# A four-layer block with deformable convolutions on one Trainium2 core: column shifts of the side convolution as transfers, the last layer's results through ScalarE

## The chip, the cores and the metric

One core of one Trainium2 chip runs the kernel, as one program written directly for the engines: TensorE (PE), VectorE (DVE), ScalarE (ACT), GpSimd (POOL) and SyncE (SP) each have their own list of instructions and meet at semaphores. The metric is the device time of one execution in microseconds (us). All data are float32.

## What is computed

The input x has shape 2 × 256 × 64 × 64 (two images, 256 channels). Four layers follow one another:

```
x = xn + proj(attention(xn)) + b,   xn = group_norm(x, 8 groups)      # layer 0
x = x + pe                                                             # layer 1
h = relu(bn1(conv1x1(x, w1)))                                          # layer 2, 64 channels
off = conv3x3(h, woff) + boff            # 27 outputs: 9 (y, x) shifts and 9 masks
h = sum_k w2[k] * bilinear(h, grid + off_k) * sigmoid(mask_k)          # 9 taps
x = relu(bn3(conv1x1(relu(bn2(h)), w3)) + x)
h = relu(group_norm(x, 32 groups))                                     # layer 3, 256 channels, twice:
off = conv1x1(depthwise7x7(h, dw), pw) + pwb                           # 18 outputs
h = sum_k w[k] * bilinear(h, grid + off_k) + b                         # 9 taps
return x + (h after the second deformable convolution)
```

## The kernel before

**Stages.** After attention (the first half of the span) there are six gather stages, each over one image of 4096 pixels in 8 groups of 512: two of 64 channels (`copies64`, `sums64`, `products64`: image 1, then image 0), two of the first 256-channel deformable convolution ("layer 0" in the code: images 1 and 0) and two of the second ("layer 1": images 1 and 0). Between them all five engines meet (`meet`), and in the meeting DVE turns the offsets into row numbers and corner weights for the next stage (`corners64`, `corners256`) and makes the group norm's statistics (`group_norm`, bn_stats on L1597, sixteen of 128x512).

**A gather stage of 256 channels.** POOL fetches, by indirect transfers from a table in DRAM, for each pixel and tap one row of four corners, 4 KB (L698). For each of 9 taps, in halves: ACT multiplies the first corner by its weight into the PSUM tensor `ps` (`products`, L1433); DVE adds the other three (`sampled`, L1979) and writes the sampled tile; PE transposes it (L1130); ACT copies the transposed tile out (`staged`, L1445); PE multiplies it with the tap's weights (L1140) and adds up nine taps in two banks of `ps`. PE needs DVE's half (`half_done`) before it transposes it; DVE needs two products of ACT (`prod_ready`) for each half. At the end of a group PE signals `o_ready`, and the result is taken out of `ps`: in layer 0 by ACT, right behind its tap 1 of the next group (`output`, L1454); in layer 1 by DVE, between the two halves of its tap 1, together with the bias and the residual in one instruction (`output`, L1966). Results leave by SP (`group_done`, L480), the residual is fetched by SP in the meeting before (L474).

**Side work.** While a stage gathers from one image, it prepares the next one: normalised rows go to a table in DRAM (ACT `side_normal`, PE `side_table3`, ACT `side_copy3`, SP `table_writes` L368, eight transfers of 64 KB a group), and the 7x7 depthwise and 1x1 convolutions, merged, give the offsets. PE multiplies all 7 rows (`side_rows3`, L1029) into 126 = 7 × 18 rows of `ps` bank 4, one for each of seven column positions and 18 outputs; DVE shifts them (`side_shifts`: one tensor_scalar L1874 and six scalar_tensor_tensor L1880, each of which picks by a 0/1 column of `sel_s` the rows of one column position, shifts them by up to three pixels and adds them into `T3`); PE sums the seven positions and brings pixels onto partitions (`side_shifted`, L976: four small matmuls); DVE adds the base grid (`side_offsets3`, L1890). The last stage (image 0, layer 1) has no side work. The 64-channel stages do the same with three column positions and 27 outputs in the first; in the second, side work is that of 256 channels for image 1.

**Order.** Each engine's list is written out by hand: `nine` for the nine taps of a group, `four` for the four tiles of 128 pixels of a group in the 64-channel stages, and `beside(n, k, ...)` places a piece of side work at tap or tile k. The side work that belongs to the group before (shifts and offsets) is done inside the next one, and behind the loop for the last. In `sums64`, DVE multiplies the gathered rows by their weights (`weigh`, L1916) three tiles ahead of the sum with the residual (`residual`, L1927). ReLU follows in the meeting (half of it `relu_half` on DVE, L2011, half on ACT), and SP spills the residual (`keep_residual`, L462).

## Time and profile before

| | |
|---|---|
| median of 3 runs | 5708.35 us (5702.64 to 5710.03) |
| profiled execution, own time | 5707.99 us |
| its span | 5705.9 us |
| PE busy | 5071.9 us, 89% |
| DVE busy | 4164.4 us, 73% |
| POOL busy | 3185.3 us, 56% |
| ACT busy | 2280.4 us, 40% |
| gathers (q0): packets, MB, share of 16 DMA engines | 193536, 679.59, 31.6% |

The span is the time between the first and the last instruction in the trace; the busy shares are averages over stages with different limits, and DMA runs only in the second half. The six gather stages lie at 2890 to 3284, 3316 to 3725, 3753 to 4228, 4257 to 4734, 4759 to 5291 and 5305 to 5703 us.

### The profile page before, as it was taken

The numbers are of one execution on the slowest core, as the hardware profiler recorded it, in microseconds if no ns is written. First come the engines' busy times: TensorE is split into PE (matmuls) and PEld (weight loads), VectorE is DVE, ScalarE is ACT, GpSimd is POOL, SyncE is SP. The second block draws the span as 40 slices with busy tenths as digits, with TensorE's granted clock in tenths as the row PEclk, the third lists the DMA queues.
The fourth block names the chain that finished last, engine by engine and source line by source line (L and its number), as shares of the span: only waits on it lengthen the run. The fifth ranks groups of instructions, "written<-read, shape, count | busy, mean of one in ns | idle before, by whom it ended". The sixth has DMA issues, their size and how long they took to land. (4 is left out here: it accounts for less than half of the span.)

```text
span 5705.9 us, 75751 instructions
## 1 busy us (share of the span) xinstructions
PE 5071.9 (89%) x23148; PEld 2362.7 (41%) x23148; DVE 4164.4 (73%) x6804; ACT 2280.4 (40%) x4146; POOL 3185.3 (56%) x2819
## 2 busy tenths in 40 slices
PE   7999999998999999999868859959968996889688
PEld 3333333333433333333346646635534553444344
DVE  4888888884588888888433333368878886877798
ACT  2444444442344444444211111135535553444455
POOL 0666666664166666666357657546635653554575
PEclk9999999999999999999978879979989997999899
DMA  2000000001000000000134344379959997897899
GB/s 71 1 1 1 1 1 1 1 1 61 1 1 1 1 1 1 1 1 1 52 99 116 92 148 149 118 288 387 378 220 369 391 370 277 323 353 296 350 409 363
DMA packets 318094, 812.22 MB, mean 142 GB/s; under 512 B 69966, under 2 KB 137428, under 8 KB 317582
## 3 DMA queue, kind: packets, MB, share of 16 engines
q0 software_dynamic: 193536, 679.59, 31.6%
q1 hardware_dynamic: 124302, 129.39, 6.7%
q8 instruction: 140, 2.29, 0.2%
q14 instruction: 116, 0.95, 0.0%
HBM read 708.40 MB, written 100.43 MB: 142 GB/s over the span
## 5 line engine op out<-in xcount | busy, mean ns | idle before, releaser
L646 POOL TENSOR_TENSOR arena<-arena 128x512 f32<-128x512 f32 x960 | 1405.4, 1464 | 829.2 <-ACT arena L1261 764.7
L1261 ACT ACTIVATE arena<-ps 128x1024 f32<-128x1024 f32 x1024 | 1048.6, 1024 | 1240.0 <-PE ps L824 1210.1
L1765 DVE TENSOR_REDUCE arena<-ps 128x2 f32<-128x1024 f32 x1024 | 1243.8, 1215 | 347.3 <-PE ps L798 347.1
L698 POOL DMA_INDIRECT arena<-corners,arena x1152 | 1084.4, 941 | 734.1 <-DVE arena L1979 360.3
L1979 DVE SCALAR_TENSOR_TENSOR ps<-arena,ps 128x256 f32<-128x256 f32 x2304 | 956.7, 484 | 273.3 <-DVEq L1973 264.1
L1140 PE MATMUL ps<-arena 128*128 128x512 f32 x2304 | 1072.2, 610 | 0.1
L824 PE MATMUL ps<-arena 64*128 64x512 f32 x4096 | 1046.5, 590 | 0.0
L837 PE MATMUL ps<-arena 128*64 128x512 f32 x4096 | 991.6, 605 | 0.0
L1787 DVE TENSOR_TENSOR arena<-arena 128x512 f32<-128x512 f32 x960 | 888.5, 926 | 62.5 <-ACT arena L1261 62.1
L682 POOL DMA_INDIRECT arena<-corners,arena x576 | 545.0, 946 | 264.2 <-issue 249.2
L1433 ACT ACTIVATE ps<-arena 128x256 f32<-128x256 f32 x1152 | 494.6, 471 | 383.5 <-DVE arena L1979 166.0
L1140 PEld LDWEIGHTS ps<-arena 128*128 128x128 f32 x2304 | 431.4, 198 | 437.5 <-issue 436.9
L1979 DVE SCALAR_TENSOR_TENSOR arena<-arena,ps 128x256 f32<-128x256 f32 x1152 | 499.8, 476 | 0.0
L824 PEld LDWEIGHTS ps<-arena 64*128 64x128 f32 x4096 | 390.9, 188 | 251.5 <-issue 169.7
L1130 PE MATMUL ps<-ident_s,arena 128*128 128x128 f32 x2304 | 335.7, 285 | 175.4 <-DVE arena L1979 163.9
L1916 DVE TENSOR_TENSOR arena<-arena,ps 128x2304 f32<-128x2304 f32 x64 | 163.5, 2554 | 438.9 <-DMA arena<-corners,arena 438.4
L1445 ACT ACTIVATE arena<-ps 128x512 f32<-128x512 f32 x576 | 309.6, 588 | 430.1 <-ACTq L1443 428.9
L837 PEld LDWEIGHTS ps<-arena 128*64 128x64 f32 x4096 | 248.9, 136 | 516.4 <-issue 339.0
L798 PE MATMUL ps<-arena 64*128 64x512 f16 x2048 | 396.6, 384 | 44.0 <-DVE arena L1765 39.2
L1130 PEld LDWEIGHTS ps<-ident_s,arena 128*128 128x128 f32 x2304 | 272.5, 145 | 338.8 <-DVE arena L1979 196.1
L798 PEld LDWEIGHTS ps<-arena 64*128 64x128 f16 x2048 | 98.7, 93 | 713.4 <-DVE arena L1765 655.7
L820 PE MATMUL ps<-arena 64*128 64x512 f16 x2048 | 389.3, 377 | 0.0
(155 smaller groups left out, 3782.1 us busy)
## 6 DMA issues: line engine op xcount, KB each, us to landing
corners<-arena SPq DMA_DIRECT2D x256, 256.0 KB
arena<-corners,arena POOLq DMA_INDIRECT x1728, 8.3
img<-in_x SPq DMA_DIRECT2D x8, 1024.0 KB, 9.3
corners<-arena SPq DMA_DIRECT2D x128, 64.0 KB, 2.2
arena<-in_wd SPq DMA_DIRECT2D x2, 2304.0 KB, 9.4
between<-img SPq DMA_DIRECT2D x4, 1024.0 KB, 5.9
arena<-between SPq DMA_DIRECT2D x4, 1024.0 KB, 9.2
resid<-img SPq DMA_DIRECT2D x4, 1024.0 KB, 7.3
```

Of the source, the lines that this page charges most:

```text
L646: pool.tensor_tensor(SUMS[u % 2][:, 0, :], SUMS[u % 2][:, 0, :], P[n % 4][:, 0, :], ALU.add).then_inc(sum_a, 1)
L682: pool.indirect_dma_start(G2[q][:, k, :], None, table64[b], bass.IndirectOffsetOnAxis(ap=IS2[:, q, k:k + 1], axis=0)).then_inc(g2_ready[q] ...
L698: pool.indirect_dma_start(G3[4 * k + t].rearrange("p a c -> p (a c)"), None, table256[b], bass.IndirectOffsetOnAxis(ap=IS3[:, k, t:t + 1], ...
L798: last = mm(ps[:, 4 + h, :], QH[u % 2][rows, t * 128:(t + 1) * 128], KH[u // QB][rows, j * CHUNK:(j + 1) * CHUNK], start=True, stop=True, ...
L824: last = mm(ps[:, 2 * (n % 2) + h, :], KF[u // QB][rows, kc * 128:(kc + 1) * 128], QF[u // QB][rows, (u % QB) * CHUNK:(u % QB + 1) * CHUNK ...
L837: last = mm(ps[64 * h:64 * h + 64, 6, :], V[:, kc, at:at + 64], P[n % 4][:, h, :], start=(kc == 0), stop=(kc == NT - 1), tile_position=(0, ...
L1130: last = tr(ps[:, 2 + half, t * 128:(t + 1) * 128], SAMP[k][:, t, half * 128:(half + 1) * 128], ident_s[:, :])
L1140: last = mm(ps[:, 6 + oh, :], WD[:, k, half, oh * 128:(oh + 1) * 128], ST[k % 3][:, half, :], start=(k == 0 and half == 0), stop=(k == KK ...
L1261: af(P[n % 4].rearrange("p h q -> p (h q)"), ps[:, 2 * (n % 2):2 * (n % 2) + 2, :].rearrange("p h q -> p (h q)"), ACT.Exp, scale=float(D) ...
L1765: v.tensor_reduce(mxp[i % 2][:, :, j], ps[:, 4:6, :], AX.X, ALU.max).then_inc(mx_done, 1)
L1787: v.tensor_tensor(SUMS[u % 2][:, 1, :], SUMS[u % 2][:, 1, :], P[n % 4][:, 1, :], ALU.add).then_inc(sum_b, 1)
L1979: last = v.scalar_tensor_tensor(SAMP[k][:, t, :] if corner == 3 else acc, G3[4 * k + t][:, corner, :], WS3[:, k, 4 * t + corner:4 * t + co ...
```

## The change

1. **Column shifts.** DVE's `side_shifts3` is gone. ACT copies the 126 rows of `ps` bank 4 into `TP3`, whose rows of pixels are three wider on each side and zero there (`side_rows_copy`; POOL clears it once), and SP issues seven transfers (`column_shifts`), each of which moves the 18 partitions of one column position, shifted, into `T3`. PE waits for all seven (`side_shifted3`), at tap 6 instead of 4.
2. **Results of the last layer.** `output` is on ACT in layer 1 too: it adds the bias and writes `OUTS` (in the memory of the attention weights); DVE adds the residual after its tap 4 (`finish`), SP sends the result then.
3. **ReLU and statistics.** `relu_half` is gone; DVE does the ReLU of the group before at tile 1 (`rectify`) and bn_stats at tile 3 (`statistics`, in `sums64`) or behind tap 4 (in `sums256`, layer 0). SP spills the residual group by group. In `sums64` DVE weighs two tiles ahead instead of three.
4. **The last group's rows** are multiplied by PE one tap or tile earlier (`at`).
5. PE, not SP, waits for the tap weights (`wd_loaded`), and DVE, behind its first group, for the residual (`residual_back`); the meetings don't.

The core of the diff:

```diff
+WP = W + 6
+T3 = off.f32(CHUNK, parts=7 * O3)
+TP3 = off.f32(8 * WP, parts=7 * O3)
...
+OUTS = wqkv_s[:, :, 0:CHUNK]
...
+    def keep_residual(b, n):
+        sp.wait_ge(rectified, CH * (n + 1))
+        sp.dma_start(resid[b][:, :, chunk(n)], INNER[b][:, :, chunk(n)]).then_inc(spilled[0], 16)
...
+    def column_shifts():
+        sp.wait_ge(rows_copied, 1)
+        sp.sem_inc(rows_copied, -1)
+        for kx in range(7):
+            at = slice(kx * O3, (kx + 1) * O3)
+            sp.dma_start(T3[at, :].rearrange("q (y x) -> q y x", x=W),
+                         TP3[at, :].rearrange("q (y x) -> q y x", x=WP)[:, :, kx:kx + W]).then_inc(shifted_in, 16)
...
-            sp.wait_ge(evicted, CH * g + oh + CH + 1)
+            sp.wait_ge(finished, CH * g + oh + 1)
...
     table_writes(0, 0, TS3, table256[0], C)
     with sp.Fori(0, NCH - 1) as g:
         table_writes(0, g + 1, TS3, table256[0], C)
+        column_shifts()
         group_done(1, g)
+    column_shifts()
     group_done(1, NCH - 1)
...
+    def side_shifted3():
+        pe.wait_ge(shifted_in, 16 * 7)
+        pe.sem_inc(shifted_in, -16 * 7)
+        pe.wait_ge(side_bank, 1)
+        pe.sem_inc(side_bank, -1)
+        for t in range(4):
+            last = mm(ps[:, 5, t * O3:(t + 1) * O3], T3[:, t * 128:(t + 1) * 128],
+                      sel3_s[:, 7:7 + O3], start=True, stop=True)
+        last.then_inc(off_ready, 1)
...
-            if k == 2 and not first:
+            at = 1 if last else 2
+            if k == at and not first:
                 side_shifts_done()
-            if k == 4 and not first:
-                side_shifted(T3[0], 7, O3, sel3_s)
-            if k >= 2:
-                side_rows3(side, n, range(2 * (k - 2), 2 * (k - 1)))
+            if k == 6 and not first:
+                side_shifted3()
+            if at <= k < at + 7:
+                side_rows3(side, n, range(2 * (k - at), 2 * (k - at + 1)))
...
+    def side_rows_copy():
+        act.wait_ge(t_ps, 1)
+        act.sem_inc(t_ps, -1)
+        af(TP3.rearrange("q (y x) -> q y x", x=WP)[:, :, 3:3 + W],
+           ps[0:7 * O3, 4, :].rearrange("q (y x) -> q y x", x=W), ACT.Copy).then_inc(side_copied, 1)
+        act.wait_ge(side_copied, 1)
+        act.sem_inc(side_copied, -1)
+        act.sem_inc(t_ready, 1)
+        act.sem_inc(rows_copied, 1)
...
+                if q == 0 and not first:
+                    side_rows_copy()
+                if q == 2 and last:
+                    side_rows_copy()
...
+        def output(g, begins=False):
...
-                af(INNER[b][:, oh, chunk(g)], ps[:, 6 + oh, :], ACT.Identity,
-                        bias=vec_s[:, B1, oh:oh + 1]).then_inc(evicted, 1)
-        def beside(n, k, ahead, last):
+                if layer == 0:
+                    af(INNER[b][:, oh, chunk(g)], ps[:, 6 + oh, :], ACT.Identity,
+                       bias=vec_s[:, B1, oh:oh + 1]).then_inc(evicted, 1)
+                else:
+                    if not begins:
+                        act.wait_ge(finished, CH * g + oh - CH + 1)
+                    af(OUTS[:, oh, :], ps[:, 6 + oh, :], ACT.Identity,
+                       bias=vec_s[:, B2, oh:oh + 1]).then_inc(evicted, 1)
+        def beside(n, k, first, ahead, last):
+            if k == 1 and not first:
+                side_rows_copy()
...
-                if k == 1 and not first and layer == 0:
-                    output(g - 1)
+                if k == 1 and not first:
+                    output(g - 1, second)
...
+        def rectify(n):
+            for half in range(CH):
+                at = chunk(n)
+                v.tensor_scalar(INNER[b][:, half, at], INNER[b][:, half, at], bn3b[:, half:half + 1], 0.0,
+                                ALU.add, ALU.max).then_inc(rectified, 1)
+        def statistics(n):
+            dve.wait_ge(rectified, CH * n + CH)
+            for half in range(CH):
+                last = v.bn_stats(bnst[:, half, bass.ds(n, 1), :].rearrange("p a b -> p (a b)"),
+                                  INNER[b][:, half, chunk(n)])
+            return last
...
-                (side_shifts2 if side == 64 else side_shifts3)()
-            if q == 2:
+            if q == 1:
+                rectify(n - 1)
+            if q == 3:
+                statistics(n - 1)
+            if q == 0 and side == 64:
+                side_shifts2()
+            if q == (2 if side == 64 else 3):
                 (side_offsets2 if side == 64 else side_offsets3)(n - 1)
 
         def four(n, first=False, last=False):
...
-                if not last or q == 0:
-                    weigh(4 * n + q + 3, n + (q + 3) // 4, (q + 3) % 4)
+                if not last or q < 2:
+                    weigh(4 * n + q + 2, n + (q + 2) // 4, (q + 2) % 4)
                 residual(4 * n + q)
                 beside(n, q, first)
-
-        for q in range(3):
+                if last and q == 2 and side == 64:
+                    side_shifts2()
...
         four(NCH - 1, last=True)
-        (side_shifts2 if side == 64 else side_shifts3)()
         (side_offsets2 if side == 64 else side_offsets3)(NCH - 1)
+        dve.wait_ge(e_free, 1)
+        rectify(NCH - 1)
...
-        def output(g):
+        def finish(g):
             for oh in range(CH):
-                dve.wait_ge(o_ready, 1)
-                dve.sem_inc(o_ready, -1)
-                if oh == CH - 1:
-                    dve.sem_inc(st_free, 1)
-                v.scalar_tensor_tensor(INNER[b][:, oh, chunk(g)], ps[:, 6 + oh, :],
-                                       vec_s[:, B2, oh:oh + 1], INNER[b][:, oh, chunk(g)],
-                                       op0=ALU.add, op1=ALU.add).then_inc(evicted, 1)
+                dve.wait_ge(evicted, CH * g + oh + CH + 1)
+                v.tensor_tensor(INNER[b][:, oh, chunk(g)], OUTS[:, oh, :], INNER[b][:, oh, chunk(g)],
+                                ALU.add).then_inc(finished, 1)
...
                 sampled(k % 3, 0)
-                if k == 1 and not first and layer == 1:
-                    output(g - 1)
                 sampled(k % 3, 1)
-                if side is not None and not first:
-                    if k == 1:
-                        side_shifts3()
-                    if k == 7:
-                        side_offsets3(g - 1)
+                if k == 4 and not first and layer == 1:
+                    finish(g - 1)
+                if k == 4 and not first and layer == 0:
+                    statistics(g - 1)
+                if side is not None and not first and k == 8:
+                    side_offsets3(g - 1)
         nine(0, first=True)
+        if layer == 1:
+            residual_back()
         with dve.Fori(1, NCH) as g:
             nine(g)
+        if side is not None:
+            side_offsets3(NCH - 1)
```

ScalarE, seventh group of a layer-0 stage before, from the tile that tap 0 left (L1445: `staged`, L1454: `output`, L1433: `products`):

```order
L1445 ACTIVATE arena<-ps 128x512 [waits st_ps,st_free]
L1445 ACTIVATE arena<-ps 128x512
L1454 ACTIVATE arena<-ps,vec_s 128x512 [waits o_ready] x2
L1433 ACTIVATE ps<-arena 128x256 [waits act_step,half_done,g_ready20]
L1433 ACTIVATE ps<-arena 128x256
L1433 ACTIVATE ps<-arena 128x256 [waits half_done,g_ready21]
L1433 ACTIVATE ps<-arena 128x256
```

And of the layer-1 stage with side work now (L1495: `staged`, L1510: `output`, L1399: `side_rows_copy`, L1483: `products`):

```order
L1495 ACTIVATE arena<-ps 128x512 [waits st_ps,st_free]
L1495 ACTIVATE arena<-ps 128x512
L1510 ACTIVATE wqkv_s<-ps,vec_s 128x512 [waits o_ready,finished] x2
L1399 ACTIVATE arena<-ps 126x8x64 [waits t_ps]
L1483 ACTIVATE ps<-arena 128x256 [waits side_copied,act_step,half_done,g_ready20]
L1483 ACTIVATE ps<-arena 128x256
L1483 ACTIVATE ps<-arena 128x256 [waits half_done,g_ready21]
L1483 ACTIVATE ps<-arena 128x256
```

The copy of 126 partitions stands between the results and the products of tap 2, whose first instruction now also waits for that copy's own end; in layer 1 the results of L1510 are new on this engine. In layer 0 the same place reads as before with the copy added.

DVE, loop of the layer-1 stage with side work, from the second of two results in tap 1 to the start of tap 2, before (L1979: `sampled`, L1966: `output`, L1874 and L1880: the shifts):

```order
L1966 SCALAR_TENSOR_TENSOR img<-ps,vec_s,img 128x512
L1966 ISA
L1966 SCALAR_TENSOR_TENSOR img<-ps,vec_s,img 128x512
L1979 SCALAR_TENSOR_TENSOR ps<-arena,ps 128x256 x4
L1979 SCALAR_TENSOR_TENSOR arena<-arena,ps 128x256 x2
L1874 TENSOR_SCALAR arena<-ps,sel_s 126x512
L1880 SCALAR_TENSOR_TENSOR arena<-ps,sel_s,arena 126x8x61
L1880 SCALAR_TENSOR_TENSOR arena<-ps,sel_s,arena 126x8x62
L1880 SCALAR_TENSOR_TENSOR arena<-ps,sel_s,arena 126x8x63 x2
L1880 SCALAR_TENSOR_TENSOR arena<-ps,sel_s,arena 126x8x62
L1880 SCALAR_TENSOR_TENSOR arena<-ps,sel_s,arena 126x8x61
L1979 SCALAR_TENSOR_TENSOR ps<-arena,ps 128x256 x4
```

The same engine now, from tap 4's second half (L2059: `sampled`, L2046 and L2047: `finish`):

```order
L2059 SCALAR_TENSOR_TENSOR ps<-arena,ps 128x256 x4
L2059 SCALAR_TENSOR_TENSOR arena<-arena,ps 128x256 x2
L2046 ISA
L2047 ISA
L2047 TENSOR_TENSOR img<-wqkv_s,img 128x512
L2046 REGISTER_ALU
L2047 ISA
L2047 TENSOR_TENSOR img<-wqkv_s,img 128x512
L2059 SCALAR_TENSOR_TENSOR ps<-arena,ps 128x256 x4
L2059 SCALAR_TENSOR_TENSOR arena<-arena,ps 128x256 x2
```

Results and shifts are gone from tap 1, and the sums with the residual stand behind tap 4. Tap 1 and tap 2 now are L2059 alone.

SyncE now, end of the loop's body in the same stage (L374: the last table write, L489: `column_shifts`, L502: results):

```order
L374 ISA
L374 DMA corners_0<-arena 64x4x256
L489 DMA arena<-arena 18x8x64 x7
L501 ISA
L502 ISA
L502 DMA out_y<-img 128x512
L501 REGISTER_ALU
L502 ISA
L502 DMA out_y<-img 128x512
```

The seven transfers stand behind the eight table writes of the next group and ahead of the two results.

## Rows read from the trace of the kernel before

**Rows 1.** Busy time by stretch: three gather stages (columns in the first row)
```profile
core 0: us, PE busy (x) PEld busy (x) DVE busy (x) ACT busy (x) POOL busy (x), PEclk, DMA share, GB/s
3753.00:4228.00 475.00, 432.82 (x1504) 229.90 (x1504) 383.82 (x927) 252.07 (x642) 271.95 (x288) 0.96 0.91 354
4759.00:5291.00 532.00, 454.59 (x1504) 239.98 (x1504) 396.09 (x944) 241.38 (x626) 269.75 (x288) 0.92 0.85 324
5302.00:5703.00 401.00, 338.13 (x1152) 171.00 (x1152) 358.97 (x880) 213.22 (x578) 269.78 (x288) 0.94 0.98 389
```

**Rows 2.** Waits, 4759 to 5291 us: total us, times, longest us
```profile
PE ps L1130 <- DVE arena L1979: 53.7, 24, 7.3
```

**Rows 3.** Waits of 3753 to 4228 us
```profile
PE ps L1130 <- DVE arena L1979: 21.2, 11, 7.3
...
ACT ps L1433 <- DMA arena<-corners,arena: 10.8, 8, 2.4
```

**Rows 4.** Timeline of PE: start us, us, instructions [idle before <-releaser]
```profile
3951.18 3.60 PE L1140 MATMUL ps<-arena 128*128 128x512 f32 x8
...
3957.60 0.66 PE L1130 MATMUL ps<-ident_s,arena 128*128 128x128 f32 x4 [1.69 <-DVE arena L1979]
...
4012.33 0.66 PE L1130 MATMUL ps<-ident_s,arena 128*128 128x128 f32 x4 [1.69 <-DVE arena L1979]
```

**Rows 5.** Busy time of one group, columns as in rows 1
```profile
3949.40:4004.10 54.70, 52.97 (x189) 28.17 (x188) 47.84 (x117) 31.39 (x80) 34.03 (x37) 1.00 0.98 383
```

**Rows 6.** Timeline of DVE, same group
```profile
3948.26 4.59 DVE L1880 SCALAR_TENSOR_TENSOR arena<-ps,sel_s,arena 126x488 f32<-126x488 f32 x6
3952.76 1.66 DVE L1979 SCALAR_TENSOR_TENSOR ps<-arena,ps 128x256 f32<-128x256 f32 x4
```

**Rows 7.** Timeline of ACT, same group
```profile
3950.31 0.69 ACT L1454 ACTIVATE img<-ps,vec_s 128x512 f32 x1 [1.09 <-ACTq L1451]
3950.90 1.66 ACT L1433 ACTIVATE ps<-arena 128x256 f32<-128x256 f32 x4
```

**Rows 8.** Timeline of PE in a group of 4759 to 5291 us
```profile
4975.84 1.01 PE L1130 MATMUL ps<-ident_s,arena 128*128 128x128 f32 x4 [2.62 <-DVE arena L1979]
4976.64 4.97 PE L1140 MATMUL ps<-arena 128*128 128x512 f32 x8
```

**Rows 9.** SP's issues of the table writes: ns min/median/max
```profile
L368 SPq DMA_DIRECT2D corners<-arena x384: 624/630/4118, 2818.2 to 5184.5; - x192
```

**Rows 10.** DMA view, 2890 to 3284 us; page: KB each, us to landing
```profile
q1 hardware_dynamic: 17408, 4.20, 4.9%
...
corners<-arena SPq DMA_DIRECT2D x128, 64.0 KB, 2.2
```

**Rows 11.** Timeline of DVE, end of the stage of 4759 to 5291 us
```profile
5282.53 0.75 DVE L1966 SCALAR_TENSOR_TENSOR img<-ps,vec_s,img 128x512 f32<-128x512 f32 x1 [1.06 <-DVEq L1963]
...
5290.88 0.23 DVE L1890 TENSOR_TENSOR arena<-ps,arena 128x72 f32<-128x72 f32 x1 [2.31 <-DVEq L1889]
...
5300.29 0.65 DVE L1738 TENSOR_TENSOR arena<-arena 128x288 f32<-128x288 f32 x1
```

**Rows 12.** Timeline of DVE, a meeting between stages
```profile
3284.55 2.35 DVE L2011 TENSOR_SCALAR img<-img,bn3b 128x4096 f32<-128x4096 f32 x1 [0.47 <-DVEq L1837]
...
3297.64 9.59 DVE L1597 BATCH_NORM_STATS2 bnst<-img 128x6 f32<-128x512 f32 x16
```

**Rows 13.** Timelines of ACT and DVE, end of the stage 3753 to 4228
```profile
4224.72 0.69 ACT L1454 ACTIVATE img<-ps,vec_s 128x512 f32<-128x512 f32 x1 [1.10 <-ACTq L1451]
...
4228.11 0.23 DVE L1890 TENSOR_TENSOR arena<-ps,arena 128x72 f32<-128x72 f32 x1 [1.49 <-DVEq L1889]
```

**Rows 14.** Timeline of ACT after the last meeting
```profile
5305.11 0.21 ACT L1422 ACTIVATE arena<-arena 128x16 f32<-128x16 f32 x1 [30.11 <-ACTq L1310]
```

**Rows 15.** Timeline of DVE, ends of the two 64-channel gather stages
```profile
3253.97 2.55 DVE L1916 TENSOR_TENSOR arena<-arena,ps 128x2304 f32<-128x2304 f32 x1 [8.07 <-DMA arena<-corners,arena]
...
3283.81 0.27 DVE L1890 TENSOR_TENSOR arena<-ps,arena 128x108 f32<-128x108 f32 x1 [2.33 <-DVEq L1889]
...
3724.58 0.23 DVE L1890 TENSOR_TENSOR arena<-ps,arena 128x72 f32<-128x72 f32 x1 [2.31 <-DVEq L1889]
```

165 lines of the change are left out of this document (88 added, 77 removed).

## The prediction

> **What bounds the kernel now.** The busy shares by stretch come first. Attention, the first half of the span, is not touched; behind it lie six stages with meetings of all engines between them. In the gather stages with side work PE is busy 433 of 475 us and 455 of 532 us; the last one, without side work, moves 389 GB/s with the DMA engines 98% busy [rows 1]. Then the waits: in the 532 us stage PE waits 53.7 us for DVE's L1979 before its transposes [rows 2], in the 475 us stage 21.2 us [rows 3]. The timeline of one group of the 475 us stage shows where: the second half of tap 2's transposes comes every 4012.33 − 3957.60 = 54.73 us, each time after a gap of 1.69 us [rows 4], the only one of its size in a group that PE fills to 52.97 of 54.70 us [rows 5]. DVE started that tap at 3952.76, after six shift instructions of 4.59 us [rows 6]. But ScalarE gave out its products for tap 2 only from 3950.90, right behind its second output L1454, which had waited for the end of PE's tap 8 [rows 7]. In the 532 us stage PE idles 2.62 us at the same place, and its next eight matmuls take 4.97 us where the first tap's eight in the other stage take 3.60 [rows 4, 8]: a lower clock after a longer stop.
>
> **Column shifts.** Per group DVE loses one L1874 and six L1880, 5.3 us. ScalarE gets one copy of ps to TP3, priced like an L1454 at 0.69 us [rows 7], with the wait for its own end 0.9 to 1.0 in all; SP gets seven transfers at 0.63 us of issue, the median of its table writes [rows 9], 4.4 us. PE takes the result at tap 6, five taps of 6 us after the copy, and SP has issued the next tables before, so the transfers are not felt inside a group. But the copy stands in ScalarE's row between output and the products of tap 2 (the rows of its order above). Worked out on the group shown: output ends at 3951.0, copy at 3951.9, products follow and DVE starts 1.0 after them (as anywhere in the loop: its start needs the first two products, 0.83), at 3952.9, where it now starts at 3952.76. So DVE is freed, then waits for ScalarE. What is late next is the thing that was late: PE's 1.69 us stay, +0.15 a group.
> The DMA engines are 98% busy in such a group, at 383 GB/s [rows 5]. Added are 7 × 18 × 8 = 1008 rows of 256 B. In the first 64-channel stage 17408 packets, nearly all of that size, took 4.9% of 16 × 394 us, 17.7 ns each [rows 10], so 1008/16 × 17.7 = 1.1 us per engine and group. They fall where POOL pauses for DVE and the queues run empty, so I take 0.3 (bounds 0 and 2.5). With the 0.15, over the 7 groups that have a predecessor, +3 for each of three stages.
>
> **Outputs of the last layer by ScalarE.** DVE no longer stands before o_ready with tap 1 and the shifts queued behind it, so the stage of 532 us becomes like the one of 475. The gap is 57 [rows 1]; about 6 of it is the tail, where two L1966 and the shifts follow one another [rows 11]. So −51; +3 as above; +2 since output transfers are squeezed into shorter groups: −46. DVE's new sums after tap 4, 2 × 0.68 by a bn_stats of that size [rows 12], lie in its slack, as do the two statistics there in the other stages. The last stage is bound by transfers, and they are the same: nothing; at its end a copy stands before DVE's sum, +0.8.
>
> **Tails of the gather stages.** The last group's rows come one tap earlier, which nothing uses: ScalarE copies them only after its output, which waits for PE's last tap. After 4225.4 [rows 13]: copy 0.9, issue 4.4, landing 2.2 [rows 10], PE's eight small matmuls 1.9 at the low clock, DVE 0.3: 4235.3 against 4228.3; then statistics of the last chunk, 1.5. That is +8.5 in each of two stages. In the third, from 5283.2 [rows 11]: 0.9 + 4.4 + 2.2 + 1.9 + 0.3 and a sum of 1.4 end at 5294.3 against 5291.1: +3.3.
>
> **Meetings.** Sixteen bn_stats, 9.59 us [rows 12], and a gap of 0.15 leave four of them, −9.7 each; the ReLU over half an image, 2.35 [rows 12], leaves two of these: −12.1 twice, −9.7 twice. ScalarE's half of the ReLU and the spill lay beside. The last meeting waited for the residual's transfers: DVE ends its corners at 5300.9, ScalarE starts at 5305.1 [rows 11, 14], where 0.4 us is what a meeting costs elsewhere. This wait moves behind DVE's first group: −3.8.
>
> **The 64-channel stages.** Two ReLUs (2.35/8 and some start, 0.35 each) and two statistics per group go to a DVE that mostly waits for gathers: nothing. DVE now multiplies two tiles ahead of its residual sums instead of three, so PE's mix 29 no longer waits behind the last multiply (3253.97). Of the first stage's tail, 3256.5 to 3284.1 [rows 15], remain: sums on PE 6, two mixes 6, shifts and offsets 3, ReLU 1, then SP's last residual transfer, 512 KB, 4 by its neighbour of 64 KB in 2.2 [rows 10] (all but the last my estimates, good to 1 each), which the meeting awaits. It ends near 3275.8: −8.3.
> In the second such stage PE is the bound with some 45 us a group. ScalarE's row copy stands before its table copy, for which PE waits: 0.4 a group, +2.5. In the last group PE asks for the shifted rows at tile 1, one tile after ScalarE's copy: copy 0.9, issue 4.4, landing 2.2, against 1 us that PE needs to get there: +6.5, and +2 for the clock. At the end copy, transfers, ReLU and spill stand in line where the shifts did: +2. Together +13 on 3724.8 [rows 15].
>
> **Sum**, against the profiled execution's 5708.0: 64-channel stages and their meetings −8.3 + 13 − 24.2 = −19.5; two gather stages 2 × (3 + 8.5 − 9.7) = +3.6; the third −46 + 3.3 − 3.8 = −46.5; the end +0.8. In all −61.6: 5646.4. The median is 0.4 above that execution, which I leave out.
>
> **Rivals.**
> *ScalarE's place does not bind.* If PE is really held by the shifts, their removal ends the 1.69 us and a group takes 53.0. For: DVE shows no idle time before tap 2. Against: the products' times [rows 7]. 2.1 less in 21 groups, −45: 5601. Chance 0.13.
> *Transfers bind.* The shifted rows come on top of engines 98% full, outside the pause, with the table writes: groups of 56.5, and 57.8 with outputs. For: 0.98 [rows 5]. Against: ScalarE waits 10.8 us for gathers in that whole stage [rows 3]. Two stages give 2 × (1.8 × 7 − 1.2) = +23, the third −51 + 3.1 × 7 − 0.5 = −30; with −19.5 and +0.8, −26: 5682. Chance 0.17.
> The Trainium skill (DMA: Bandwidth & Descriptors, section on why a DMA increments its semaphore by 16) says that a transfer runs on as many engines, at most 16, as divide its slowest dimension; 18 partitions would use 9. No row here shows engines apart; by it nine engines get 2.0 us a group instead of 1.1, an estimate, which speaks for this rival.
> *Slower: short rows cost like long ones.* The mechanism: each of the 1008 rows of 256 B holds an engine as long as a gathered row of 4 KB, which at 383 GB/s over 16 engines is 171 ns. 63 rows per engine make 10.8 us a group, 9.5 beyond the pause: 14 × 9.5 − 2.4 in two stages, −51 + 7 × 9.8 − 0.5 in the third, with −18.7 for the rest +129: 5837. It decides from 3.4 us net a group, 74 ns a row. Against: 17.7 ns [rows 10]. Chance 0.05.
> The skill's same page (Specifications) puts the line rate at 512 B and more, with a read-modify-write below. The trace's 17.7 ns are 14 GB/s an engine, under the gathers' 24: it agrees in sign, not in a size that would decide.
> *It does not do what it says*: PE's stops in the third stage have another cause and stay, only the rest counts, +3.6 + 3 − 19.5: near 5695. Chance 0.03.
>
> **Numbers.** Forecast 0.62: 5646.4, its own range 5625 to 5668 from ±1 us in 21 groups. Full gain and transfers reach from 5601 to 5682, and the tails are sure to no better than 8 us: 5603 to 5688. 0.2% is 11.4 us, about what a measurement of this kernel can tell from no change: faster 0.93, same 0.02, slower 0.05.
>
> **What would show it.** Right: the third gather stage near 489 us; ScalarE's copy to TP3 right before the products of tap 2, PE's gap before tap 2's second transposes 1.7 to 2 us in all three stages; 7 us more from ScalarE's last output to DVE's last offsets; no sixteen statistics behind the corners; in the second 64-channel stage a stop of PE of 6 to 7 us in the last group. Wrong: groups of 53 us; ScalarE waiting for gathers in every group; PE waiting for the shifted rows at tap 6.

## The result, and the profile after

The changed kernel took 5669.14 us, median of 4 runs (5668.3 to 5672.7), the kernel before 5708.33 (5702.64 to 5710.03, 4 runs): a ratio of 0.9934, 95% interval 0.9922 to 0.9946. The change is faster by 39 us where 62 were forecast. Its profiled execution has a span of 5668.2 us, 37.7 under the one before. One execution of one kernel below (DVE's shifts with offsets at tile 2) took 8915 us at a clock of 0.55 where its other three took 6321 to 6325, and is left out there.

The six stages, each from ScalarE's first instruction in it to its first in the next (so with the meeting behind it), in us:

| stage | before | after | change | forecast |
|---|---|---|---|---|
| first 64-channel | 425.9 | 412.9 | −12.9 | −20.4 |
| second 64-channel | 437.1 | 466.1 | +29.0 | +0.9 |
| layer 0, image 1 | 503.9 | 503.0 | −0.9 | +1.8 |
| layer 0, image 0 | 501.9 | 498.4 | −3.5 | +1.8 |
| layer 1, image 1 | 545.9 | 496.0 | −49.9 | −46.5 |
| layer 1, image 0 | 400.8 | 401.9 | +1.1 | +0.8 |

The busy times of the second 64-channel stage, of the first and third gather stage with side work and of the last one (columns as in [rows 1]):

```profile
3303.00:3751.00 448.00, 365.16 (x2080) 281.15 (x2080) 121.40 (x167) 76.96 (x184) 272.67 (x288) 0.87 0.46 135
3769.00:4252.00 483.00, 432.99 (x1504) 230.12 (x1504) 352.92 (x887) 257.03 (x650) 272.11 (x288) 0.95 0.93 352
4770.00:5252.00 482.00, 433.88 (x1504) 230.26 (x1504) 354.71 (x887) 259.30 (x650) 274.88 (x288) 0.95 0.95 363
5266.00:5668.00 402.00, 335.19 (x1152) 164.87 (x1152) 357.71 (x880) 221.91 (x594) 272.53 (x288) 0.97 0.98 389
```

The third gather stage with side work has lost its 50 us and looks like the first. The last one is as it was. The loss is in the first line: 448 us where the kernel before took 408.5, PE's granted clock at 0.87. Before, the same stage read:

```profile
3316.00:3725.00 409.00, 342.22 (x2080) 263.37 (x2080) 146.38 (x192) 72.56 (x177) 272.36 (x288) 0.93 0.45 134
```

**Where the second 64-channel stage lost it.** PE's timeline of one group before (L1021: table transposes, L1042: sums of products):

```profile
3540.51 0.63 PE L1021 MATMUL ps<-ident_s,arena 128*128 128x128 f32 x4 [0.72 <-PEq L1017]
3540.98 3.74 PE L1042 MATMUL ps<-ident_s,arena 128*128 128x128 f32 x32
...
3548.46 0.66 PE L1021 MATMUL ps<-ident_s,arena 128*128 128x128 f32 x4
3548.95 3.74 PE L1042 MATMUL ps<-ident_s,arena 128*128 128x128 f32 x32
```

And now (L1051: table transposes, L1072: sums, L1006: the small matmuls with the shifted rows, L1059: rows), with DVE's two instructions that end the wait:

```profile
3534.88 1.09 PE L1051 MATMUL ps<-ident_s,arena 128*128 128x128 f32 x4 [2.46 <-PEq L1047]
3535.76 6.14 PE L1072 MATMUL ps<-ident_s,arena 128*128 128x128 f32 x32
...
3546.53 0.63 PE L1051 MATMUL ps<-ident_s,arena 128*128 128x128 f32 x4 [0.78 <-PEq L1047]
3546.99 5.37 PE L1072 MATMUL ps<-ident_s,arena 128*128 128x128 f32 x32
...
3533.33 1.28 DVE L2001 BATCH_NORM_STATS2 bnst<-arena  x2
3534.52 0.21 DVE L1952 TENSOR_TENSOR arena<-ps,arena 128x72 f32 x1
```

PE stops twice ahead of its table transposes, 2.46 and 0.78 us. The first stop ends with DVE's offsets (L1952), which give back bank 5 and now stand at tile 3 behind the statistics (L2001). The second ends with ScalarE's first table copy, which stands behind the new row copy. The 32 matmuls behind each stop, 3.74 us before at a granted clock of 1.00, take 6.14 and 5.37: the granted clock is 0.59 and 0.69 over them, so they run at the lower of the two clock levels for part of their time. A group takes 52.0 us between two of DVE's offsets, mean of six, where it took 45.3.

The sixth of these intervals ends in the last group, where PE asks for the shifted rows at tile 1, one tile after ScalarE's copy:

```profile
3707.22 1.86 PE L1006 MATMUL ps<-sel_s,arena 126*128 126x18 f32 x8 [7.90 <-PEq L1004]
3708.92 9.21 PE L1059 MATMUL ps<-img,arena 128*126 128x512 f32 x14
```

PE stops 7.90 us, and the 14 row matmuls behind it take 9.21 us where they took 6.25. Counted on PE, between the table transposes of the groups, the stage splits like this: 4.6 us less up to the second group, 28.8 more in the next five groups (46.5 to 52.2 us each), 13.7 more from there to the last offsets.

**A group of layer 0**: PE (L1051: table transposes, L1161: transposes), ScalarE (L1505: result, L1399: row copy, L1483: products) and DVE (L2059), to be held against [rows 4, 6, 7]:

```profile
4026.33 0.63 PE L1051 MATMUL ps<-ident_s,arena 128*128 128x128 f32 x4 [0.85 <-PEq L1047]
...
4028.58 0.85 PE L1161 MATMUL ps<-ident_s,arena 128*128 128x128 f32 x4 [1.19 <-DVE arena L2059]
...
4021.01 0.69 ACT L1505 ACTIVATE img<-ps,vec_s 128x512 f32 x1 [1.09 <-ACTq L1501]
4021.60 0.60 ACT L1399 ACTIVATE arena<-ps 126x512 f32<-126x512 f32 x1
4022.72 1.67 ACT L1483 ACTIVATE ps<-arena 128x256 f32<-128x256 f32 x4 [0.52 <-ACTq L1477]
...
4023.74 0.88 DVE L2059 SCALAR_TENSOR_TENSOR ps<-arena,ps 128x256 f32<-128x256 f32 x2 [5.47 <-DVEq L2053]
```

The order is the one forecast: result, row copy, 0.52 us of waiting for the copy's own end, then the products. DVE, freed of the shifts, waits 5.47 us. PE's one stop of 1.69 has become 0.85 (ahead of its table transposes) and 1.19. Over six groups the mean is 55.24 us where it was 54.78, and in the stage of image 0 it is 55.04 where it was 54.78; the loop's period differs from group to group, so single groups say little. In none of these groups does PE wait for the shifted rows; it does so only at the ends of stages.

**The end of that stage**, after ScalarE's last result [rows 13]:

```profile
4240.09 0.69 ACT L1505 ACTIVATE img<-ps,vec_s 128x512 f32<-128x512 f32 x1 [1.10 <-ACTq L1501]
4240.68 0.60 ACT L1399 ACTIVATE arena<-ps 126x512 f32<-126x512 f32 x1
...
4241.55 6.09 SPq L489 DMA_DIRECT2D arena<-arena  x7
...
4249.39 1.86 PE L1006 MATMUL ps<-sel_s,arena 126*128 126x18 f32 x8 [9.50 <-PEq L1004]
...
4251.41 0.23 DVE L1952 TENSOR_TENSOR arena<-ps,arena 128x72 f32<-128x72 f32 x1 [24.09 <-DVEq L1951]
```

Copy, seven issues in 6.09 us, landing, small matmuls, offsets: 10.9 us from result to offsets, where 2.9 were before, so 8.0 more.

### The profile page after: what moved, and what is told of

Same layout as the page of the kernel before. It is cut to its first block and busy times, and to the rows that moved or that the text cites. A ratio compares the mean times of both kernels' runs of the same rounds, so it can differ in the third digit from the quotient of the medians.

```text
span 5668.2 us, 75917 instructions
## 1 busy us (share of the span) xinstructions
PE 5075.3 (90%) x23148; PEld 2371.7 (42%) x23148; DVE 4010.8 (71%) x6610; ACT 2315.8 (41%) x4208; POOL 3194.0 (56%) x2820
## 5 line engine op out<-in xcount | busy, mean ns | idle before, releaser
L2059 DVE SCALAR_TENSOR_TENSOR ps<-arena,ps 128x256 f32<-128x256 f32 x2304 | 955.8, 482 | 350.2 <-DVEq L2053 339.7
L1171 PE MATMUL ps<-arena 128*128 128x512 f32 x2304 | 1046.8, 598 | 0.2
L698 POOL DMA_INDIRECT arena<-corners,arena x576 | 545.9, 948 | 299.4 <-issue 245.7
L1483 ACT ACTIVATE ps<-arena 128x256 f32<-128x256 f32 x1152 | 497.2, 470 | 403.7 <-DMA arena<-corners,arena 193.5
L2059 DVE SCALAR_TENSOR_TENSOR arena<-arena,ps 128x256 f32<-128x256 f32 x1152 | 498.3, 473 | 0.0
L1161 PE MATMUL ps<-ident_s,arena 128*128 128x128 f32 x2304 | 333.0, 282 | 134.4 <-DVE arena L2059 122.1
L1495 ACT ACTIVATE arena<-ps 128x512 f32<-128x512 f32 x576 | 309.1, 587 | 319.9 <-ACTq L1493 319.6
L1161 PEld LDWEIGHTS ps<-ident_s,arena 128*128 128x128 f32 x2304 | 269.1, 144 | 300.0 <-DVE arena L2059 156.9
```

Source lines behind the costliest of these rows:

```text
L698: pool.indirect_dma_start(G2[q][:, k, :], None, table64[b], bass.IndirectOffsetOnAxis(ap=IS2[:, q, k:k + 1], axis=0)).then_inc(g2_ready[q] ...
L1161: last = tr(ps[:, 2 + half, t * 128:(t + 1) * 128], SAMP[k][:, t, half * 128:(half + 1) * 128], ident_s[:, :])
L1171: last = mm(ps[:, 6 + oh, :], WD[:, k, half, oh * 128:(oh + 1) * 128], ST[k % 3][:, half, :], start=(k == 0 and half == 0), stop=(k == KK ...
L1483: af(ps[:, h, (t % 2) * C:(t % 2 + 1) * C], G3[4 * k + t][:, 0, :], ACT.Copy, scale=WS3[:, k, 4 * t:4 * t + 1]).then_inc(prod_ready, 1)
L2059: last = v.scalar_tensor_tensor(SAMP[k][:, t, :] if corner == 3 else acc, G3[4 * k + t][:, corner, :], WS3[:, k, 4 * t + corner:4 * t + co ...
```

## The experiments

All changes below are made to the changed kernel. The first four ran on one chip, with the kernel before at 5706.4 us (7 runs). Of the other eight, four ran on a second chip and four on a third, on which the gathers were slower: the kernel before took 6413.0 and 6447.7 us there. Times of these are compared inside their set, and ratios are with the kernel before of the same set. The changed kernel itself was not run on the second and third chip, and stage times come from one execution each.

### Offsets at tile 2

```
-                    if q == (2 if side == 64 else 3):
+                    if q == 2:
                         (side_offsets2 if side == 64 else side_offsets3)(n - 1)
```

> One line: in the second 64-channel stage DVE does the offsets at tile 2 again, not behind the statistics of tile 3. Theory A (the 29 us that this stage gained are PE's stops ahead of the table transposes, 2.46 and 0.81 us a group, and the lower clock after them): the first stop goes back to 0.7, the clock comes back for part of the group, the stage from start to start falls from 466 to 443 (435 to 450), the time from 5669 to 5646. Theory B (DVE weighs two tiles ahead instead of three, and PE waits for it): only the stop itself goes, 6 times 1.7, the stage stays above 455, 5659.

Measured: 5652.75 us (5649.47 to 5653.88), ratio 0.9906 (0.9889 to 0.9922). The stage takes 446.0 us instead of 466.1, inside the 435 to 450 of theory A and under the 455 of theory B. PE's timeline:

```profile
3524.39 0.63 PE L1051 MATMUL ps<-ident_s,arena 128*128 128x128 f32 x4 [0.72 <-PEq L1047]
...
3534.85 0.63 PE L1051 MATMUL ps<-ident_s,arena 128*128 128x128 f32 x4 [0.81 <-PEq L1047]
```

The stop of 2.46 is back at 0.72, the second is unchanged. The stage fell by 20 us, twice the 1.74 times 6 of the stops alone. The rest is the clock: PE is busy with the same matmuls for 354.7 us of the stage instead of 365.2.

### Row copy behind the first table copy

```
+                        if q < 2 and not last:
+                            side_copy3(q)
                         if q == 0 and not first:
                             side_rows_copy()
                         if q == 2 and last:
                             side_rows_copy()
-                        if q < 2 and not last:
-                            side_copy3(q)
```

> ScalarE's row copy stands behind its first table copy in that stage instead of ahead of it. Theory A: the second stop, 0.81 us, goes in six groups and with it a part of the lower clock: the stage 466 to 455, 5658. If only the first stop brings the clock down: 5 us less at most, 5664. Theory B: 5664 too.

Measured: 5665.1 us (5661.07 to 5668.19), ratio 0.9927 (0.9911 to 0.9944), the stage 461.2. The second stop is gone, and the matmuls behind the first take 4.78 us instead of 6.14. But the copy comes later, and so do the seven transfers behind it, and now PE waits for the shifted rows at tile 2 in each of these groups, 1.22 to 1.98 us, which it did not in the changed kernel:

```profile
3551.49 1.04 PE L1006 MATMUL ps<-sel_s,arena 126*128 126x18 f32 x8 [1.59 <-PEq L1004]
3552.38 7.95 PE L1059 MATMUL ps<-img,arena 128*126 x14
```

So the 5 us are the balance of one stop removed and another one made, and not the price of the second stop alone.

### Column shifts on DVE again

```
+                        if side is not None and not first and k == 1:
+                            side_shifts3()
...
-                pe.wait_ge(shifted_in, 16 * 7)
-                pe.sem_inc(shifted_in, -16 * 7)
...
-                    if k == 6 and not first:
+                    if k == 4 and not first:
                         side_shifted3()
```

and `side_rows_copy` and `column_shifts` left out in all places, DVE's shifts put in at tile 0 of the 64-channel stage and at the ends.

> Column shifts back on DVE in all four stages, all else as in the change (offsets of the last group behind the shifts). What the transfers bought or cost. My forecast's step (ScalarE's place in its row binds, not DVE's shifts): gather groups stay at 54.6 us within 0.4, the tails of the three gather stages are 7 to 8 us shorter each, the second 64-channel stage about 5 shorter, since the row copy and the transfers at its end are gone: 5669 - 29 = 5640. Rival (the shifts did hold PE): groups of 55.5 or more, 21 of them, +20, less the tails: 5665.

Measured: **5604.49 us** (5603.35 to 5605.24), ratio 0.9823 (0.9806 to 0.9839), 65 us under the changed kernel and 36 under the 5640 expected. Its stages, in the order of the table: 411.9, 438.7, 490.4, 487.3, 482.3, 401.7. So the transfers, with ScalarE's copy that feeds them, cost 27 us in the second 64-channel stage, where 5 were expected, and 12.6, 11.1 and 13.7 in the three gather stages. Groups take 54.72 us in the stage of image 1 of layer 0 and in that of layer 1, where the transfers add 0.5 each; in the stage of image 0 they take 54.97, and the transfers add 0.1. Most of the gain in the gather stages is at their ends: from the last offsets of the loop to the last ones of the stage it is 12.96 us, where the changed kernel takes 24.3 in layer 0 and 22.5 in layer 1. PE's timeline in the two kinds of stage (L1039: table transposes, L1149: transposes):

```profile
3520.89 1.08 PE L1039 MATMUL ps<-ident_s,arena 128*128 128x128 f32 x4 [2.34 <-PEq L1035]
...
3999.85 0.66 PE L1149 MATMUL ps<-ident_s,arena 128*128 128x128 f32 x4 [1.69 <-DVE arena L2044]
...
4054.58 0.66 PE L1149 MATMUL ps<-ident_s,arena 128*128 128x128 f32 x4 [1.69 <-DVE arena L2044]
...
3991.27 3.83 DVE L1922 SCALAR_TENSOR_TENSOR arena<-ps,sel_s,arena 126x496 f32<-126x496 f32 x5
3995.01 1.66 DVE L2044 SCALAR_TENSOR_TENSOR ps<-arena,ps 128x256 f32<-128x256 f32 x4
...
3993.15 1.66 ACT L1467 ACTIVATE ps<-arena 128x256 f32<-128x256 f32 x4
```

PE's 1.69 us in layer 0 are exactly those of [rows 4]. The last three lines tell what I had decided too fast: DVE starts tap 2 at 3995.01, right when its own last shift ends (3991.27 + 3.83 = 3995.10), and ScalarE's first two products had been there since 3994.0. In the changed kernel DVE starts 1.02 us after ScalarE begins its products (4022.72 to 4023.74), which here would have been 3994.2. So the shifts hold DVE, and by 0.8 us; behind them ScalarE's chain is the next. The change took away the first chain and made the second one longer by a row copy and its wait, 0.60 + 0.52 us, and so gave back the whole 0.8. In the 64-channel stage PE still stops 2.34 us a group (the offsets are at tile 3 here too), but groups take 47.8 us.

### Half of tap 2's products ahead of the results

```
-                        products(3 * g + k // 3, k % 3)
+                        products(3 * g + k // 3, k % 3, (1,) if k == 2 and not first else (0, 1))
...
                         if k == 1 and not first:
+                            products(3 * g, 2, (0,))
                             output(g - 1, second)
...
```

> ScalarE gives out the first half of tap 2's products before the two results and the row copy instead of behind them. If ScalarE's place in its row binds a gather group: PE's stop of 1.19 us ahead of tap 2's second transposes goes, groups fall from 54.6 to 53.4 or a little less, 20 groups, 5669 - 24 = 5645. If the DMA engines bind (1.01 busy in such a group): groups stay within 0.3, 5665 to 5670, and ScalarE waits for gathers instead.

Measured: 5643.53 us (5640.93 to 5646.02), ratio 0.9891 (0.9875 to 0.9908). The two sides of the expectation are each right in one kind of stage. Groups of layer 0 fall from 55.24 to 53.38 (image 0: 55.04 to 53.30) and their stages to 488.6 and 486.8: there ScalarE's place in its row did bind. In layer 1 groups stay at 55.19 us (495.3 the stage). A stretch of layer 0 of this kernel, and who waits in its layer-1 stage:

```profile
3980.00:4035.00 55.00, 55.00 (x194) 29.05 (x193) 46.29 (x115) 33.39 (x85) 35.15 (x38) 1.00 1.03 399
...
ACT ps L1484 <- DMA arena<-corners,arena: 47.1, 29, 2.5
```

The same wait in the layer-1 stage of the changed kernel and of the one with DVE's shifts:

```profile
ACT ps L1483 <- DMA arena<-corners,arena: 32.4, 19, 2.8
...
ACT ps L1467 <- DMA arena<-corners,arena: 4.3, 2, 2.4
```

The engines of DMA are full in this stretch of layer 0, at 399 GB/s. Over the six groups of the loop both layers move 386 GB/s here at a DMA share of 1.01, and a group of layer 1 sends its results on top; in the changed kernel layer 0 moved 373, and layer 1 already 384 at the same share of 1.01. So the changed kernel had room left in layer 0 and next to none in layer 1. ScalarE's wait for gathers is 47.1 us in this layer-1 stage, but 56.5 in the layer-0 stage, where the kernel gained, so the length of that wait alone does not tell the two apart. That is the rival "transfers bind", half true: transfers hold layer 1 at about its present 55.2 us a group, and not at the 57.8 that the rival gave.

### Transfers doubled

```
-                for kx in range(7):
+                for to, kx in [(to, kx) for kx in range(7) for to in (T3B, T3)]:
...
-                pe.wait_ge(shifted_in, 16 * 7)
+                pe.wait_ge(shifted_in, 16 * 14)
```

> The changed kernel with each of the seven transfers sent twice (the second time to a place that nothing reads), PE waiting for all fourteen. If the transfers' load on the DMA engines costs (the rival of short rows, or engines that are full): each gather group of layer 0 and of layer 1 grows by as much as the first seven cost, 0.5 us or more. If only the issue time and the landing at the ends cost, groups stay within 0.3 us and each of the four tails grows by seven issues, 4.4 to 6 us: 5669 + 22 = 5691. If short rows cost like long ones, 21 groups grow by 9 us: 5860.

On the second chip: 6369.44 us (6346.42 to 6373.47), ratio 0.9918 (0.9892 to 0.9944). And again:

> The doubled transfers again, for the same reason as above. On an undisturbed chip: groups of layer 0 from 55.2 to 55.5 or less if the transfers' load is small beside the gathers, tails 5 us longer each, 5691; groups over 56 if it costs as much as the first seven or more, 5703 or above.

On the third chip: 6407.62 us (6403.84 to 6408.4), ratio 0.9935 (0.992 to 0.9951). On both chips gathers were slow, so neither set answers for the first chip. What can be read is the end of each layer-0 stage, where no gathers run: 30.7 us from the loop's last offsets to the stage's last ones in both sets (image 1), where one set of seven took 24.3. Seven more issues cost 6.3 us, 0.9 each. Inside groups the two kernels with single transfers on the second chip (the next two experiments) can be held against it: layer 0 takes 68.9 us against 66.0 and 65.5 for image 1, but 66.2 against 67.1 and 65.9 for image 0. These single ones differ by up to 1.2 us among themselves where their gather loops are the same, so seven more transfers cost between nothing and some 3 us a group while gathers are slow; what they cost beside full-speed gathers stays open. It is nothing like the 9.5 us of short rows that cost as long ones.

### Row copy of the last group at tap 8

```
-                    if k == 1 and not first:
+                    if (k == 1 and not first) or (k == 8 and last):
                         side_rows_copy()
...
                 output(NCH - 1)
-                if side is not None:
-                    side_rows_copy()
```

> In the last group of each gather stage with side work ScalarE copies the rows at tap 8, as soon as they are there, instead of behind the last results. If the tail is this chain (copy, seven issues, landing, small matmuls): it falls by 8 us in two stages, and by 4 in the third, where the results' transfers end last: 5669 - 20 = 5649. If something else holds the tail: 5666 to 5670.

On the second chip: 6266.87 us (6259.95 to 6280.69), ratio 0.9775 (0.9755 to 0.9795). The end of a layer-0 stage:

```profile
4547.70 0.60 ACT L1399 ACTIVATE arena<-ps 126x512 f32<-126x512 f32 x1 [3.98 <-ACTq L1398]
...
4555.52 0.69 ACT L1505 ACTIVATE img<-ps,vec_s 128x512 f32<-128x512 f32 x1 [1.10 <-ACTq L1501]
...
4548.59 6.09 SPq L489 DMA_DIRECT2D arena<-arena  x7
...
4556.42 1.04 PE L1006 MATMUL ps<-sel_s,arena 126*128 126x18 f32 x8 [1.10 <-PEq L1004]
...
4557.62 0.23 DVE L1950 TENSOR_TENSOR arena<-ps,arena 128x72 f32<-128x72 f32 x1 [14.86 <-DVEq L1949]
```

The transfers now run while PE is at the last taps, and its stop ahead of the small matmuls is 1.10 us instead of 9.50. From the loop's last offsets it is 15.1 us instead of 24.3 in layer 0, and 15.3 instead of 22.5 in layer 1: 9 and 7 us, where 8 and 4 were expected. This is the forecast's step on the tails, seen from the other side: the rows come one place earlier, and the copy has to use it.

### Results of layer 1 on DVE again

```
                         sampled(k % 3, 0)
+                        if k == 1 and not first and layer == 1:
+                            output(g - 1)
                         sampled(k % 3, 1)
-                        if k == 4 and not first and layer == 1:
-                            finish(g - 1)
```

> Results of layer 1 on DVE again, between its two halves of tap 1, all else as in the change (shifts by transfers). What ScalarE's output is worth in the third gather stage. My forecast took the stage's whole gap (51 us) for DVE standing before the results with tap 1 and the shifts behind: without the shifts, tap 1's second half alone is late, by about 5 us less 2.6 of slack, groups 57.5 to 58.5: 496 + 18 = 514 for the stage, 5687 in all. If the results alone were the cause, the stage goes back to 540 or more, 5713.

On the second chip: 6305.76 us (6296.06 to 6314.77), ratio 0.9832 (0.981 to 0.9853). Held against the kernel of the run before, which differs in its ends alone in the other stages: groups of layer 0 65.5 and 66.0 us, of layer 1 68.25 and 64.74. The results on DVE cost 3.5 us a group, 25 in the stage, against 2.3 to 3.3 a group expected; layer 0 of image 0, where the two gather loops are the same, shows 65.9 and 67.1, so this figure is good to about 1 us. With the shifts on DVE too, the kernel before took 62.16 against 54.78, 7.4. The run with the shifts back on DVE gives the other side of it: with the results moved to ScalarE and the shifts not moved, a group of layer 1 takes 54.72 us on the first chip. So moving the results was enough for the whole gain of the third stage, and the shifts added nothing to it; had the shifts alone been moved, about half of the 7.4 would have stayed. That half comes from a chip with slower gathers and is rough.

### DVE's shifts with offsets at tile 2

```
-                    if q == (2 if side == 64 else 3):
+                    if q == 2:
```

(on the kernel with DVE's shifts)

> Column shifts on DVE (as in the run that took 5604.5) and DVE's offsets of the second 64-channel stage at tile 2. Theory A (PE's stop of 2.34 us ahead of the table transposes, and the lower clock after it, are what is left of that stage's loss): its groups fall from 47.8 to the 45.3 of the kernel before, the stage from 438.7 to 421, the time from 5604 to 5587. Theory B (weighing two tiles ahead holds groups above 45.3): 47 and more, 5598 or above.

On the second chip: 6321.18 us (6320.68 to 6325.06, 3 runs), ratio 0.9852 (0.9831 to 0.9873). And again:

> The kernel with DVE's shifts in one piece and offsets at tile 2 again, since the first set with it ran where gathers were slower. As stated there: second 64-channel stage from 438.7 to 421 if PE's stop and the clock behind it are what is left of its loss, 5587 in all, 0.979 of the kernel before; 5598 if weighing two tiles ahead holds it.

On the third chip: 6363.75 us (6354.24 to 6370.59), ratio 0.9873 (0.9856 to 0.9889). Neither answers the question: the second 64-channel stage takes 555 and 560 us on these chips, and in none of the kernels there under 555, since gathers are slow. Whether its groups would come back to 45.3 us stays open. They show something else. On the second chip the layer-0 stage of image 1 takes 605.2 us, where the two kernels with transfers took 578.5 and 582.0; that of image 0 takes 587.9 against 583.1 and 584.6. On the first chip DVE's shifts had been better by 12.6 and 11.1.

### DVE's shifts in two parts

```
                         if side is not None and not first and k in (1, 2):
                             side_shifts3(k - 1)
...
+                            products(3 * g, 2, (0,))
                             output(g - 1, second)
```

> Shifts on DVE, but in the 256-channel stages in two parts: four instructions behind tap 1, three behind tap 2 (in the loop; at the end in one piece), ScalarE's first half of tap 2's products ahead of the results, and the offsets of the second 64-channel stage at tile 2. If PE's 1.69 us stop ahead of tap 2's second transposes is DVE's and ScalarE's lateness only, it goes in 21 groups: 54.73 to 53.3 or less, 30 us under the same kernel with the shifts in one piece: 0.977 of the kernel before or less (5575 to 5560 where that takes 5706). If the DMA engines (98% busy) bind right behind, layer 0 gains a part and the stage with results nothing: 0.979 or more.

On the third chip: **6280.2 us** (6275.4 to 6287.19, 5 runs), ratio **0.9742** (0.9728 to 0.9756), 83 us under the kernel with shifts in one piece, which also lacks the second edit, half of tap 2's products ahead of the results. The same layer-0 stage of both, the one piece first, and how long POOL waited for DVE to free the buffers of the gathers:

```profile
3992.00:4585.00 593.00, 477.56 (x1504) 249.72 (x1504) 398.10 (x952) 252.03 (x640) 272.77 (x288) 0.88 0.78 284
...
POOL arena L704 <- DVE arena L2044: 198.3, 32, 10.9
```

```profile
3992.00:4560.00 568.00, 461.50 (x1504) 243.32 (x1504) 399.01 (x954) 251.19 (x640) 272.00 (x288) 0.91 0.81 296
...
POOL arena L704 <- DVE arena L2067: 143.2, 33, 9.0
```

POOL waits 55 us less for DVE and the gathers move 296 GB/s instead of 284. Groups take 67.7 us instead of 70.1. The gain is larger than the 30 us of PE's stops. A likely reason is that seven instructions in a row on DVE hold back the next gathers for 5.3 us, and that this time is lost where gathers are the bound. The rows go with it but don't prove it: the kernel differs in two edits, and no run has one of them alone. That two parts also take away PE's 1.69 us on a chip with fast gathers was expected and not measured.

### Everything mended, with transfers

Four of the edits shown above in one kernel: offsets at tile 2, the row copy behind the first table copy, half of tap 2's products ahead of the results, the last group's row copy at tap 8.

> Shifts by transfers as in the change, with everything mended that the runs pointed at: offsets at tile 2, row copy behind the first table copy, first half of tap 2's products ahead of the results, row copy of the last group at tap 8. If the transfers themselves are cheap and only the places around them were bad, it comes out level with or under the kernel with DVE's shifts: 5669 - 25 - 26 - 20 = 5598, 0.981 of the kernel before. If the transfers cost in the groups that are full, the stage with results stays at 55 us a group, and it ends over DVE's version by 10 us or more.

On the third chip: 6308.0 us (6300.99 to 6336.32), ratio 0.9797 (0.9773 to 0.9821). That is 56 us under DVE's shifts in one piece on the same chip and 28 over those in two parts. The layer-0 stages are level with the two parts (579.8 and 573.4 against 580.5 and 578.3); the stage with results takes 604.3 against 578.6, and the second 64-channel stage 568.1 against 559.4. It would fit that transfers lose where they come on top of results on their way out. But on the second chip the kernel with transfers and the copy at tap 8 took 562.0 us for the stage with results, and the one with DVE's shifts in one piece 598.3. In this stage the kernel here differs from the first of these by half the products ahead, and by the chip; which of the two makes the 604.3 is open.

### Two kinds of chip

The last stage has no side work and is nearly the same in every kernel after the change (one has its results on DVE, three half of tap 2's products ahead). It takes 401.6 to 402.0 us on the first chip and 535 to 548 on the others. Here it is in the kernel with DVE's shifts on the first chip, and in the one with offsets at tile 2 besides on the third, where its instructions are the same:

```profile
5201.00:5600.00 399.00, 335.51 (x1152) 165.37 (x1152) 357.56 (x880) 221.64 (x592) 273.03 (x288) 0.97 0.98 391
```

```profile
5808.00:6350.00 542.00, 369.22 (x1152) 197.77 (x1152) 352.13 (x880) 222.26 (x592) 276.58 (x288) 0.82 0.77 288
```

DVE and ScalarE are busy for the same time within 2%, and the gathers move 391 GB/s in one and 288 in the other.

## Why the prediction was right, and where it was not

The sign and the range held: 5669 lies in 5603 to 5688. The number missed by 23 us, and the likeliest case's own range of 5625 to 5668 by 1. That the total is no further off is in part luck, since steps missed in both directions: 28 us too hopeful in the second 64-channel stage and 7.5 in the first, 3 to 5 too careful in each of the three gather stages. By its steps:

**Outputs of the last layer: right.** −49.9 against −46.5. That "the stage of 532 us becomes like the one of 475" is what happened: groups of 55.24 us in both layers. The sum is nearer than its parts: the stage itself took 482 us where 489 were given as the sign, and the meeting behind it gained 0.6 where −3.8 was forecast. And the run with the shifts back on DVE shows that the results alone were the cause.

**Column shifts in gather groups: right in size, half right in reason.** +0.46 us a group was measured where 0.45 was forecast (+0.26 in the stage of image 0), and ScalarE's copy stands where it was said to: "DVE is freed, then waits for ScalarE" is in the rows. That the two figures agree so closely is luck, since of the 0.45 two thirds were the load of the transfers, which no run measured beside full-speed gathers. The other third came out because two amounts of about 1 us nearly cancel. Before, it was the shifts that held DVE: they end at 3948.26 + 4.59 = 3952.85 [rows 6], and DVE starts at 3952.76, 0.8 us later than ScalarE's products of 3950.90 [rows 7] would have let it. So "for" in the rival "ScalarE's place does not bind" was true of the kernel before, and the rival is refuted for the changed one, by the half products, 1.9 us a group in layer 0: with both out of the way a group takes 53.4 us, near the rival's 53.0. "Transfers bind" is refuted in its size (56.5 and 57.8 us a group against 55.2), and for layer 0 as a whole; in layer 1 they leave no room for a further step. The Trainium skill's rule that a transfer issued by SP runs on as many engines, at most 16, as divide its slowest dimension (DMA: Bandwidth & Descriptors, the section on why a DMA increments its semaphore by 16) was not decided: no run tells engines apart. The same section of the Trainium skill says that the issuing sequencer itself writes what the unused engines don't count. In the trace a transfer of 18 partitions takes SP 0.839 us to issue, median of 224, and a table write of 64 partitions 0.657; the section gives no time for that write, and the two transfers differ in shape as well, so no run here shows whether it is the cause.

**Tails of the gather stages: right.** 10.9 us from result to offsets against 9.9 forecast and 2.9 before; the issues took 6.1, not 4.4, since an issue costs 0.9 and not 0.63 us. The price was taken from a row of another shape. The statement that the rows' earlier place is something "which nothing uses" was right for this change, and was its missed chance: with the shifts on DVE, which can start as soon as the rows are there, the end takes 12.96 us, and with the copy at tap 8 15.1, where the kernel before took 23.3.

**Meetings: right**, −8.8 in the layer-0 ones, where −9.7 for the statistics and +1.5 for those of the last chunk were forecast. The last one was forecast to lose its wait for the residual, −3.8. It lost it, and gained 3.29 us of waiting. SP waits there for the transfers of the last results, which it issued up to 5253.45, and DVE goes on at 5256.19: a wait took the place of the one removed, which the forecast had asked of other steps and not of this one.

**The first 64-channel stage: too hopeful by 7.5.** The terms of its end add up to 3276.5 and not to the 3275.8 given, which is 0.7 of it. The tail behind the last multiplication holds two tiles' sums on PE and not one, and the meeting waits 2.40 us for SP's last residual where it waited 0.47.

**The second 64-channel stage: the step that failed.** The forecast gave "ScalarE's row copy stands before its table copy, for which PE waits: 0.4 a group, +2.5". It measured +28.8 in five groups alone, 5.8 each. The last group came out nearly as forecast: PE's stop there was 7.90 us where 6.5 was given, and the slower clock behind it cost 3.0 where 2 was. Two things were missed in the groups. DVE's offsets moved from tile 2 to tile 3, behind the statistics, and they give back the bank that PE needs first thing in the next group: this was in the order of the instructions and I priced the statistics at nothing, "a DVE that mostly waits for gathers", without asking who waits for what stands behind them. And a stop of PE was priced at its own length. In this stage PE is the bound, and behind the stops the granted clock fell: 3.74 us of matmuls took 6.14. With the offsets at tile 2 the stage fell by 20 us, with the shifts back on DVE by 27; the two overlap, and were not measured together where gathers are fast.

## What to carry to other kernels

Taking work off an engine helps only if its start is not also set by another chain: before moving it, look at what else ends at the moment where the engine starts again, and price the case in which the other chain gets longer. When a release (a bank, a buffer) is moved behind other work on an engine that mostly waits, ask who waits for the release and how fast the waiting engine is afterwards; behind a stop of 2.5 us on PE the next 32 matmuls took 1.0 us longer where it stood alone and 2.4 where a second, shorter stop followed in each group. Work that goes to another engine's row and through transfers also lengthens the end of each stage, where nothing hides it: 9.5 to 11.5 of the 11 to 14 us that it cost here in a gather stage. Where gathers were slow, a long run of small instructions on the engine that frees gather buffers did best cut in two and spread, together with half of tap 2's products moved ahead (0.9742 of the kernel before, against 0.9797 for transfers on the same chip); which of the two edits brought it was not separated.

## What the runs showed of the hardware

The same kernel, on three chips, took 5706, 6413 and 6448 us. In the traces of its variants the difference lies behind attention: the first gather stage starts at 2888 to 2892 us on all three, and the last stage moved 391 GB/s on one and 288 on another. The trace does not show why. The Trainium skill (HBM Reference, Specifications (TRN2)) says that the two cores of a memory domain share its bandwidth; no run here shows the other core. The order of two variants can turn with it: shifts by transfers lost 12.6 and 11.1 us in the two layer-0 stages against DVE's where gathers were fast, and on the second chip they won 23.2 and 3.3 (605.2 against 582.0, 587.9 against 584.6). On the third they won 27.0 and 28.5 (606.8 against 579.8, 601.9 against 573.4), with half the products ahead and the copy at tap 8 besides.

Issuing a transfer of 18 partitions with 8 rows of 256 B each took SP 0.84 us and its next one followed after 0.9, where the 64-partition table writes took 0.63 to 0.66 each with 256 rows against 144.
